# Four of the first loads move to ScalarE's DMA queue, and the last stores alternate between two queues: a fused group norm, quantised grouped 1x1 convolution and residual

## The reference

```python
def _gn(v, G=32, eps=1e-05):
    ...
    return ((g - m) / jnp.sqrt(s + eps)).reshape(v.shape)
...
identity = x
perm = jnp.concatenate([jnp.arange(1, G), jnp.arange(1)])
xg = x.reshape(B, G, Cg, H, W)[:, perm]
xa = jnp.clip((xg - lA) / (uA - lA), 0.0, 1.0)
xa = ste_round(xa * (ACT_LEVELS - 1)) / (ACT_LEVELS - 1)
...
y = jnp.einsum('bgihw,goi->bgohw', xa, wg).reshape(B, C, H, W)
y = y * inv[None, :, None, None] + (beta - running_mean * inv)[None, :, None, None]
y = jax.nn.relu(y)
return y + identity
...
x = x + _L0_conv_ref(_gn(x), ...)
```

## Time and profile before

| | |
|---|---|
| time, median of 3 runs | 259.81 us (259.12 to 260.0) |
| the profiled execution's own time | 259.98 us |
| its span | 258.3 us |
| busy, share of the span | PE 74%, DVE 89%, ACT 83%, POOL 83% |
| DMA | 103.28 MB, mean 400 GB/s |
| mean granted TensorE clock | 0.906 of full speed |

### The profile page before, as it was taken

How to read it: one execution, slowest core, us unless ns; L and a number is a source line. 1 busy time by engine, 2 the same in 40 slices (tenths; PEclk the granted TensorE clock), 3 DMA queues, 4 the chain that set the end, 5 groups by cost and what they waited for, 6 DMA issues and landing times.

```text
span 258.3 us, 4030 instructions
## 1 busy us (share of the span) xinstructions
PE 190.6 (74%) x999; PEld 109.4 (42%) x999; DVE 229.5 (89%) x363; ACT 215.4 (83%) x394; POOL 213.5 (83%) x340
## 2 busy tenths in 40 slices
PE   1142995987788898668598787979966878998930
PEld 0132654553444555344364444454633535464410
DVE  2898698799999989999979999998999998999950
ACT  4338898889999998999978999989899997989600
POOL 6126869998999999899999999999989999989500
PEclk9999997699979779999859997986999995999995
DMA  6999999999999999999999999999999999999994
GB/s 216 394 413 411 409 407 410 415 415 419 416 417 415 413 416 417 413 417 418 412 417 417 416 418 417 412 415 416 415 417 417 416 413 408 402 399 393 381 385 158
DMA packets 34520, 103.28 MB, mean 400 GB/s; under 512 B 1202, under 2 KB 1730, under 8 KB 34498
## 3 DMA queue, kind: packets, MB, share of 16 engines
q1 hardware_dynamic: 18624, 54.86, 53.5%
q10 hardware_dynamic: 15874, 48.18, 46.8%
HBM read 51.65 MB, written 51.38 MB: 399 GB/s over the span
## 4 chain that ended last, share of the span: by engine, by line
POOL 35%; DVE 21%; PE 20%; issue 17%; DMA 2%; DVEq 1%; SPq 0%; POOLq 0%; ACT 0%
POOL images L411 17%; PE prod L594 14%; DVE images L482 9%; DVE stats L456 7%; POOL levels L421 6%; PE var_ps L584 5%; POOL dev L372 3%; DVE codes L471 3%; DMA images<-in_x 2%; POOL norm L399 1%; POOL dev L375 1%; POOL newt L395 1%; POOL scaled L401 1%; POOL newt L396 1%; POOL newt L397 1%
## 5 line engine op out<-in xcount | busy, mean ns | idle before, releaser
L594 PE MATMUL prod<-codes,w_t 128*128 128x392 bf16 x768 | 155.6, 357 | 18.1 <-DVE images L482 11.9
L482 DVE SCALAR_TENSOR_TENSOR images<-prod,floor,images 128x784 f32<-128x784 f32 x128 | 127.9, 1020 | 11.0 <-PE prod L594 10.8
L411 POOL TENSOR_SCALAR images<-images,coef 128x784 f32<-128x784 f32 x120 | 128.6, 1083 | 0.0
L594 PEld LDWEIGHTS prod<-codes,w_t 128*128 128x128 bf16 x768 | 76.4, 107 | 88.8 <-issue 43.1
L267 ACT ACTIVATE levels<-images,coef 128x784 int16<-128x784 f32 x95 | 91.5, 1028 | 0.4 <-POOL coef L403 0.4
L456 DVE BATCH_NORM_STATS2 stats<-images 128x6 f32<-128x392 f32 x136 | 68.9, 551 | 5.2 <-DMA images<-in_x 5.2
L240 ACT ACTIVATE unused<-images,sums 128x784 bf16<-128x784 f32 x60 | 56.1, 938 | 0.1
L234 ACT ACTIVATE unused<-images 128x784 bf16<-128x784 f32 x60 | 50.7, 846 | 6.2 <-DMA images<-in_x 5.1
L471 DVE TENSOR_SCALAR codes<-levels 128x3136 bf16<-128x3136 int16 x32 | 34.2, 1070 | 1.0 <-POOL levels L421 1.0
L421 POOL TENSOR_SCALAR levels<-images,coef 128x784 int16<-128x784 f32 x33 | 32.9, 997 | 0.1
L584 PE MATMUL var_ps<-dev,avg 128*128 128x8 f32 x128 | 21.9, 299 | 14.5 <-POOL dev L379 14.5
(11 more groups left out here) (66 smaller groups left out, 80.1 us busy)
## 6 DMA issues: line engine op xcount, KB each, us to landing
images<-in_x SPq DMA_DIRECT2D x30, 1568.0 KB, 13.2
out<-images ACTq DMA_DIRECT2D x30, 1568.0 KB, 17.5
images<-in_x SPq DMA_DIRECT2D x8, 392.0 KB, 6.6
out<-images SPq DMA_DIRECT2D x1, 1568.0 KB, 8.6
out<-images SPq DMA_DIRECT2D x4, 392.0 KB, 6.5
w_raw<-in_weight SPq DMA_DIRECT2D x1, 256.0 KB, 6.4
rows<-in_channel_params ACTq DMA_DIRECT2D x1, 8.0 KB, 2.4
limit_row<-in_limits ACTq DMA_DIRECT2D x1, 0.0 KB
```

The source lines that it names most:

```text
L411: nc.gpsimd.tensor_scalar(here, here, coef[:, u % 2, 0, 1, G * j + o:G * j + o + 1], coef[:, u % 2, 1, 1, G * j + o:G * j + o + 1], ALU.mu ...
L482: nc.vector.scalar_tensor_tensor(out=two, in0=prod[:, k % SETS, :, 0:HALF], scalar=floor[:, o:o + 1], in1=two, op0=ALU.max, op1=ALU.add).t ...
L594: done = nc.tensor.matmul(prod[:, k % SETS, h, 0:HALF], w_t[:, part, output_group(g)], codes[:, n % 2, g, h * HALF:(h + 1) * HALF], start= ...
```

## The change

Images 5, 7, 9 and 11 are no longer loaded by SyncE. ScalarE issues their loads from its own queue, between its statistics of images 0 to 3. SyncE goes from image 4 to image 6 and so on. The stores of images 25, 27 and 29 move from ScalarE's queue to SyncE's, the store of image 30 from SyncE's to ScalarE's, and of the four pieces of image 31 the first and third stay on SyncE's queue and the second and fourth go out on ScalarE's. No compute instruction is added, removed or moved against the others of its engine.

```diff
+ACT_LOADS = (5, 7, 9, 11)
+BOTH_STORE = 25
...
+        def stored_by_act(n):
+            return n < BOTH_STORE or n % 2 == 0
+
+        def store_group(engine, g):
+            o, j = output_group(g), (B - 1) % RING
+            engine.wait_ge(final, G * (B - 1) + g + 1)
+            engine.dma_start(out_v[B - 1][:, o], images[:, j, o]).then_inc(stored[j], DMA)
...
             for n in range(SINGLE, B):
-                load(n)
-            for n in range(ACT_STORES, B - 1):
-                store(n)
-            for g in range(G):
-                o = output_group(g)
-                sync.wait_ge(final, G * (B - 1) + g + 1)
-                sync.dma_start(out_v[B - 1][:, o], images[:, (B - 1) % RING, o]).then_inc(stored[(B - 1) % RING], DMA)
+                if n not in ACT_LOADS:
+                    load(n)
+            for n in range(BOTH_STORE, B - 1):
+                if not stored_by_act(n):
+                    store(n)
+            for g in range(0, G, 2):
+                store_group(sync, g)
...
             def store(n):
-                if 0 <= n < ACT_STORES:
+                if n >= 0 and stored_by_act(n):
...
+            def load(n):
+                act.dma_start(images[:, n], x_v[n]).then_inc(x_loaded[n], DMA)
+
             image_stats(0)
+            load(ACT_LOADS[0])
             image_stats(1)
             copy_mean(0)
+            load(ACT_LOADS[1])
             image_stats(2)
             deviation(0)
+            load(ACT_LOADS[2])
             image_stats(3)
+            load(ACT_LOADS[3])
...
+            store(B - 2)
+            for g in range(1, G, 2):
+                store_group(act, g)
```

More of the change, by code:

```diff
@@ L24 @@
 HELPED = 4
-ACT_STORES = 30
+ACT_LOADS = (5, 7, 9, 11)
+BOTH_STORE = 25
 SETS = 3
```

## The result

The changed kernel takes 263.12 us in the median of 4 runs (262.42 to 264.57), against 259.53 us before (259.12 to 260.0, 4 runs). The ratio is 1.0137, with a 95% interval of 1.0111 to 1.0163: slower by 1.4%. The forecast was 264.0 us. The profiled execution took 263.48 us, of which 261.8 us are its span.

What follows compares the result with a forecast made beforehand. A compute chain and a nearly never idle DMA stream, nearly equally long, bound the kernel. Span 258.3 + 5.7 (late start) - 1.5 (tail) = 262.5, + 1.68 around it = 264.2, median 0.17 lower: 264.0 us; range 259.2 to 267.5.

Steps and rivals of the forecast that it cites:

- The share of the second queue: At the start: ScalarE's loads get half the traffic, beginning 3.7 us after the issue, from about 10 us on.
- The near images: At the start: images 2, 3 and 4 land at 21.0, 26.8 and 34.5 us instead of 17.1, 21.0 and 24.9.
- the three slower cases: Images 2 and 3 alone, 262.1 us, chance 0.22; the forecast, 263 to 265.5, 0.44; image 4's stall undamped, 267.5, 0.12.
- Image 4's stall: VectorE waits 2.1 us for image 4; the second `finish`'s 2.44 us wait for TensorE absorbs that extra.
- The hole in the stream: After the first loads and store: DMA engines idle for 3.5 to 5 us, and 1 us more at the next store.
- the wait of the second store: In the middle: the second store, issued at 55.7 us, has its bytes from 59.3.
- The chain carries the delay to the end: From the start to the last `finish`: the compute chain stays 5.7 us late, ending at about 254.4 us.
- The tail's 1.5 us: At the end: two store queues, refilled gaps and a faster last landing gain 1.5 us as a whole.
- The sum: Whole kernel: 258.3 + 5.7 - 1.5 = 262.5 us of span, giving a 264.0 us median.
- the rival with images 2 and 3 alone: At the start: image 7's load comes too late to touch image 3; 3.8 us delay, 262.1 us, chance 0.22.

Runs made afterwards that it cites:

- late far loads: Changed kernel, but ScalarE's four loads are images 8, 9, 10 and 11, all issued behind the statistics of image 3; ratio 1.0156 to the kernel before.
- changed again: The changed kernel measured once more, unaltered, on another chip than the first comparison; 264.32 us, ratio 1.0201 to the kernel before.
- loads only: Changed kernel with only its four loads on ScalarE's queue, all stores as in the kernel before; ratio 1.0121 to the kernel before.
- stores-only: Changed kernel with only its alternating stores from image 25 on, all loads on SyncE's queue as before; ratio 1.0014 to the kernel before.
- order on SyncE: Changed kernel with no ScalarE loads; SyncE issues the first whole loads as 5, 2, 7, 3, 9, 4, 11, 6, 8, 10; ratio 1.0171 to before.
- only image 5: Changed kernel with only image 5's load on ScalarE's queue, stores as in the changed kernel; ratio 1.0039 to the kernel before.
- ScalarE late, 3 and 9: Two runs: kernel before plus three or nine idle activations on ScalarE ahead of quantising image 0, transfers untouched; ratios 1.0034 and 1.0145.
- ScalarE late, 6: Kernel before plus six idle activations on ScalarE between image 3's statistics and quantising image 0, transfers untouched; ratio 1.0066.

## Why the prediction was right, point by point

- **The share of the second queue** was right: half each, 3.6 us after the issue.
- **The near images.** Forecast for the statistics of images 2 and 3, `cap(0)` and image 4's stats: 21.0, 26.8, 30.8, 34.5. Measured: 20.52, 27.53, 31.45, 35.39. The first store was forecast at 45.5 and issued at 45.13. Of the three slower cases that of the forecast is what happened. Image 4's stall was absorbed as argued: the first `finish` started 8.1 us later (37.28 against 29.18), the second 5.5 (38.2 against 32.66).
- **The hole in the stream** was forecast as 3.5 to 5 us of idle engines between 54.3 and 59.3 and 1 us more. By the rate it was 3.2 us from 52 to 68. By the engines' busy share, 0.92 against 1.03, they were idle for only (1.03 - 0.92) / 1.03 x 16 = 1.7 us; the rest is a lower rate while busy, which the prediction didn't have and no run explains. Mis-sized was the wait of the second store: it was given the 3.7 us that the first store had behind running loads. Issued at 55.29 to idle engines, it moved 412 GB/s from 56.3 on, 1 us later. The first store landed at 57.2, not 55.9; the load of image 12, issued at 57.2 while the second store was running, had its first bytes at about 61, again some 3.7 us later.
- **The chain carries the delay to the end**: right in its number (254.4 forecast, 254.77 measured), not borne out as a rule. From the first store to the last `finish` the profiled execution before took 209.0 us, the others 205.3 (late far loads) to 210.9 (changed again); in loads only a delay of 4.7 us had shrunk to 2.0. What makes this pace differ is open: there is one profiled execution of each kernel, and of the changed one two, with 209.6 and 210.9 us. That it differed by only 0.7 us from before in the changed kernel's execution is luck.
- **The tail's 1.5 us** was mis-sized: the alternation is worth nothing (1.0014, 0.9995 to 1.0034), neither in the rate nor in the gaps. What did come off at the end, 8.7 to 6.3 us for the last piece, comes with the late chain's smaller backlog: the same stores had 9.0 us to land in the stores-only run.
- **The sum.** Forecast 262.5 of span, measured 261.8; forecast 264.0 us, measured 263.12. The terms were 5.7 and -1.5; measured were 6.0 and -2.4, the second for another reason than the alternation. The time alone doesn't tell the forecast from its neighbour, the rival with images 2 and 3 alone at 262.1; the start of image 3's statistics and of the first store do.

Shown: a first store that is some 5 us late (4.7 to 6.0), and with it the whole chain, cost this kernel 1.2 to 2.0% in all six comparisons, whatever makes it late: loads in the wrong order on either queue, ScalarE held at an issue, or idle work on ScalarE. Not separated: how the loss reaches the end. The changed kernel (both profiled executions), order on SyncE, only image 5 and ScalarE late, 3 and 9 ended with the chain, less the 2 us or so by which the last piece landed faster. Loads only, late far loads and ScalarE late, 6 ended with the stream, later than before by 2.0, 3.8 and 0.6 us, where it had lost 1.7, 3.6 and 1.0 in the middle. A start some 5 us late brings both, and no run has one without the other.

## What to carry to other kernels

Where transfers and compute are nearly balanced, the time to protect at the start is that of the first store: until it lands, a ring of buffers has nothing more to load, and the DMA engines run dry. Loads that are needed late must then not be put beside the near ones on a queue of their own, since the two queues are served half and half and the far images take the near ones' bandwidth; order the loads by their use. A second queue added no bandwidth here, and an engine that computes should not issue several large transfers in a row. And look at how long the last store takes to land: near the time that a store takes on a free queue (6.4 us for 392 KB here), compute sets the end; well above it, the stream does.

## What the runs showed of the hardware

- Behind a busy queue, a transfer on the other queue waits some 3.6 us for its first bytes (6.41 to 10 us, and 39.77 to 43.5 for a full half before), and then has half of the engines at once. With idle engines it had the full rate after 1 us (issued at 55.29, 412 GB/s from 56.3 on).
- An issue can hold its engine: of four loads of 1568 KB in a row the first two took 0.96 us, the next two 7.13, and the fourth alone 6.57. In the changed kernel, where image 5 had landed (12.1 us after its issue at 6.41) before the fourth was issued at 28.52, each of the four took 0.37 to 0.46.
- Rates of this kernel's streams: loads alone 407 to 413 GB/s, on one queue or two; stores alone 400, on one queue or two; both together 416.
